# Routed expert blocks: conditional weight loads and stores, and a new pairing of blocks, in a four-layer kernel on one core

## Chip, core and metric

The kernel runs on one core of one Trainium2 chip. The metric is the device time of one execution in microseconds (us). Five engines work side by side: TensorE (PE, matmuls; its weight loads are shown as PEld), VectorE (DVE), ScalarE (ACT), GpSimd (POOL) and SyncE (SP, which here only issues DMAs). Each follows its own list of instructions and meets the others through semaphores. DMAs are issued from the queues of SP, ACT and POOL and move data between the large memory (HBM) and the on-chip memory (SBUF). A change is called a change here if it moves the time by more than about 1%, which is what a measurement of this kernel tells from no change.

## What is computed

The input is 8 sequences of 256 tokens with 256 features, 2048 tokens in all. Four layers follow each other, each inside `x = x + layernorm(layer(layernorm(x)))`: causal attention with 16 heads, a mixture of experts, an mLSTM, and a feed-forward layer with a 2:4 sparse hidden vector. The change lies in the mixture of experts:

```python
_, topk_idx = jax.lax.top_k(logits + router_bias, K)          # K = 4 of E = 64 experts
topk_scores = jnp.take_along_axis(scores, topk_idx, axis=-1)
topk_scores = topk_scores / (topk_scores.sum(-1, keepdims=True) + 1e-08)
combine = jnp.zeros((n, E)).at[jnp.arange(n)[:, None], topk_idx].add(topk_scores)
h = silu(einsum('nd,edf->enf', flat, Wg)) * einsum('nd,edf->enf', flat, Wu)     # F = 64
out = einsum('enf,efd->nd', h * combine.T[:, :, None], Wd)
for i in range(2):                                            # shared experts
    out = out + (silu(flat @ Sg[i]) * (flat @ Su[i])) @ Sd[i]
```

Only the 4 chosen experts of a token have a weight other than zero in `combine`, so 2048 x 4 = 8192 rows have to go through an expert.

## The kernel before, in words

All five engines' lists are written by hand, and no scheduler orders anything. The attention layer comes first (up to about 280 us of the profile), then the router and the shared experts, then the routed experts (363 to 580 us), then the mLSTM and the feed-forward layer.

**Blocks.** The router gives every expert as many blocks of 128 rows as its rows need. The blocks of all experts lie one behind the other, and there is room for XB = 128 of them. Block k belongs to expert `ebrow[k]`; `rows_at[:, k]` holds the token of each of its 128 rows, or a number outside the table where there is none. The blocks in use are the first ones; those behind are empty, and `ebrow` gives the last expert for them. How many are in use is known only at run time, in the last place of `upto`. For the inputs of the reference the rows per expert, counted from the reference's own formulas, make 96 blocks in use and 32 empty ones.

**Pairs.** The routed stage is a loop over XPAIR = 64 pairs of blocks, here called pair 0 to pair 63; pair i holds blocks 2i and 2i+1, so that pairs 0 to 47 are full and pairs 48 to 63 are empty. All 64 are computed in full. For each pair:

- SP loads the experts' weights, two DMAs of 192 KB (`expert_weights`, L405 and L406: read the expert's number from `ebrow` into a register, then issue). There are WRING = 7 buffers; the load for pair i waits until the second matmul step of pair i-7 is done (`e_dn`).
- POOL gathers the token rows, two indirect DMAs (L529), from `xnd` in HBM into a ring `xg` of RING = 4 pairs; the gathers for pair i wait for the transposes of pair i-4 (`e_xt`). Rows outside the table are not moved.
- PE transposes the rows (L1298, `e_xt`), ACT copies the result out of PSUM (L782, `e_xc`), PE does gate and up (L1310, `e_gu`), ACT takes the silu (L798, `e_sg`), DVE multiplies (L1999, `e_h`), PE does the down product (L1321, `e_dn`), DVE copies it to `ysb` (L2006, `e_y`).
- ACT stores the 256 rows of the pair to `yd` in HBM with one DMA of 256 KB (`expert_rows`, L787). `ysb` is a ring of 4 pairs: DVE's copy waits for the store of four pairs before (`e_o0` to `e_o3`).

PE's order is: transposes of i+1, gate and up of i, down of i-1. ACT's is: copy of i+1, silu of i, store of i-2.

After the loop POOL waits for all stores and gathers each token's four rows from `yd` (L545, the first at 583.9 us), while PE finishes the shared experts.

**Earlier on SP.** During the attention layer SP stores the normalized input of each sequence to `xnd` (L391, eight DMAs of 256 KB, the first at 87.6 us, the last at 276.0 us). The gathers wait for all eight (`x_st`).

## Time and profile before

| | us |
|---|---|
| three runs | 970.70, 972.15, 979.53 |
| their median | 972.15 |
| span of the profiled execution | 1017.7 |
| of it the stretch 363 to 580, the routed experts | 217 |

The profiled execution is an execution of its own and was 45.5 us longer than the median of the unprofiled ones. Share of the span in which each engine was busy: PE 85%, PEld 71%, DVE 66%, ACT 38%, POOL 39%. The granted clock of PE has the mean 0.892 of its full speed over the span.

How to read it: "busy" counts the engine's instructions, not its waits. A busy PE is not a PE at its best, because ends of matmuls are modelled. "Issue" is idle time in which the profile shows nothing that the engine waited for. The name behind an arrow is what ended the wait, "remote" or "another core or an unknown queue" one that the profile can't name.

### The profile page before, as it was taken

How to read it: one execution, taken by the hardware profiler on the slowest of the kernel's cores; microseconds unless marked ns; L12 is line 12 of the kernel's file. 1: busy time of each engine (PE TensorE's matmuls, PEld its weight loads, DVE VectorE, ACT ScalarE, POOL GpSimd, SP SyncE). 2: the span in 40 equal slices, each digit the busy share in tenths (PEclk: the TensorE clock that was granted, in tenths of full speed). 3: DMA queues.
4: the chain of work that ended last, by engine and by line, in shares of the span. 5: the costliest groups of instructions: out<-in, count | busy, mean ns of one | idle time of the engine just before them, and what ended most of it. 6: DMA issues, size and time to landing. Idle time of an engine off the chain costs nothing.

```text
span 1017.7 us, 18542 instructions
## 1 busy us (share of the span) xinstructions
PE 862.2 (85%) x6718; PEld 722.4 (71%) x6718; DVE 667.7 (66%) x1500; ACT 389.5 (38%) x764; POOL 396.7 (39%) x548
## 2 busy tenths in 40 slices
PE   4899899898688857667777859899999999999994
PEld 3777777776576846556666748778788888788883
DVE  6567777765577615885444547668778865867875
ACT  2244444444433713232222325435555564222220
POOL 3123333323432266766565283466665322100001
PEclk9799999998899968998898977758888887999997
DMA  7000000000000248888876551221111000000001
GB/s 248 2 1 13 12 12 9 5 12 12 22 1 22 87 136 260 250 257 242 242 222 184 162 178 52 82 59 52 46 42 41 0 1 1 0 1 21 22 1 41
DMA packets 59384, 77.66 MB, mean 76 GB/s; under 512 B 9746, under 2 KB 51997, under 8 KB 59304
## 3 DMA queue, kind: packets, MB, share of 16 engines
q1 hardware_dynamic: 32040, 40.92, 13.1%
q0 software_dynamic: 9856, 18.92, 6.9%
q10 hardware_dynamic: 17408, 16.78, 4.7%
q8 instruction: 47, 0.77, 0.3%
q14 instruction: 33, 0.27, 0.1%
HBM read 61.88 MB, written 23.07 MB: 83 GB/s over the span
## 4 chain that ended last, share of the span: by engine, by line
PE 43%; DVE 12%; issue 5%; another core or an unknown queue 4%; ACT 3%; POOL 2%; DMA 1%; ACTq 0%; POOLq 0%; DVEq 0%
PE S L1310 5%; PE S L1298 4%; PE S L959 3%; PE S L961 3%; PE S L960 3%; PE S L944 3%; PE ZO L1518 2%; PE ZO L1321 2%; PE T L1321 2%; PE T L1518 2%; PE ZO L1431 2%; DVE work L1566 1%; PE ZO L1433 1%; PE ZO L1432 1%
## 5 line engine op out<-in xcount | busy, mean ns | idle before, releaser
L529 POOL DMA_INDIRECT work<-xnd,rows_at x128 | 134.8, 1053 | 87.6 <-issue 38.6
L446 POOL TENSOR_SCALAR veps<-mv 128x2 f32<-128x2 f32 (+1 forms) x63 | 15.6, 247 | 287.8 <-DVE mv L1561 287.6
L1999 DVE TENSOR_TENSOR work<-work,S 64x256 f32<-64x256 f32 x128 | 54.2, 424 | 83.0 <-ACT work L798 52.9
L455 POOL TENSOR_SCALAR_AFFINE_SELECT work<-work 128x256 f32<-128x256 f32 x128 | 53.7, 444 | 118.0 <-ACT work L650 118.0
L959 PE MATMUL ZO<-parts 128*128 128x256 f32 x224 | 71.4, 319 | 16.6 <-DVE parts L1600 6.4
L959 PE MATMUL S<-xr,parts 128*128 128x512 f32 x192 | 83.5, 435 | 0.8 <-issue 0.8
L960 PE MATMUL S<-xr,parts 128*128 128x512 f32 x192 | 77.5, 404 | 0.0
L961 PE MATMUL S<-xr,parts 128*128 128x512 f32 x192 | 77.5, 403 | 0.0
L782 ACT ACTIVATE work<-S 128x512 f32<-128x512 f32 x64 | 38.2, 597 | 100.7 <-PE S L1298 43.5
L650 ACT ACTIVATE work<-S 128x768 f32<-128x768 f32 x64 | 51.7, 812 | 55.5 <-PE S L1033 55.5
L960 PE MATMUL ZO<-parts 128*128 128x256 f32 x224 | 66.3, 296 | 0.0
L961 PE MATMUL ZO<-parts 128*128 128x256 f32 x224 | 66.2, 295 | 0.0
L1033 PE MATMUL S<-parts 32*128 32x256 f32 (+1 forms) x768 | 57.9, 288 | 4.8 <-DVE parts L1626 3.8
L959 PEld LDWEIGHTS ZO<-parts 128*128 128x128 f32 x224 | 45.3, 202 | 21.9 <-issue 9.3
L1310 PE MATMUL S<-work,raw 128*128 128x128 f32 x296 | 46.7, 309 | 10.8 <-issue 10.7
L545 POOL DMA_INDIRECT attn_w<-yd,slots x44 | 49.8, 1131 | 11.9 <-issue 11.9
L1298 PE MATMUL S<-ident,work 128*128 128x128 f32 x256 | 47.4, 314 | 8.2 <-DMA work<-xnd,rows_at 8.2
L1033 PEld LDWEIGHTS S<-parts 32*128 32x128 f32 x768 | 48.9, 191 | 7.1 <-DVE parts L1626 5.0
L1310 PEld LDWEIGHTS S<-work,raw 128*128 128x128 f32 x296 | 42.5, 221 | 13.0 <-issue 12.9
L447 POOL TENSOR_TENSOR rstd<-veps,mhalf 128x2 f32<-128x2 f32 (+1 forms) x63 | 48.1, 763 | 5.2
L798 ACT ACTIVATE work<-S 64x256 f32<-64x256 f32 x64 | 24.1, 377 | 59.1 <-remote 30.8
L960 PEld LDWEIGHTS ZO<-parts 128*128 128x128 f32 x224 | 45.8, 205 | 0.1
(330 smaller groups left out, 2355.7 us busy)
## 6 DMA issues: line engine op xcount, KB each, us to landing
yd<-work ACTq DMA_DIRECT2D x64, 256.0 KB
raw<-in_experts SPq DMA_DIRECT2D x74, 192.0 KB
work<-in_experts SPq DMA_DIRECT2D x36, 192.0 KB
lg_all<-in_experts SPq DMA_DIRECT2D x18, 192.0 KB
xnd<-attn_w SPq DMA_DIRECT2D x8, 256.0 KB, 2.1
shd<-work SPq DMA_DIRECT2D x8, 256.0 KB, 2.3
work<-xnd,rows_at POOLq DMA_INDIRECT x128
raw<-in_ffn SPq DMA_DIRECT2D x2, 1024.0 KB, 5.4
```

The lines of the kernel that those rows point to most:

```text
L447: pool.tensor_tensor(rstd[:, 0:n], veps[:, 0:n], mhalf[:, 0:n], ALU.pow).then_inc(s["ln_rs"], 1)
L455: last = pool.affine_select(out=diagonal, in_=diagonal, compare_op=ALU.is_ge, fill=0.0, base=0, pattern=[[0, 2], [1, P]], channel_multipli ...
L529: pool.indirect_dma_start(xg[:, i % RING, b, :], None, xnd[:], bass.IndirectOffsetOnAxis(ap=rows_at[:, 2 * i + b:2 * i + b + 1], axis=0), ...
L545: pool.indirect_dma_start(gathered(b, t, k), None, yd[:], bass.IndirectOffsetOnAxis(ap=slots[:, 2 * b + t, k:k + 1], axis=0)).then_inc(s[" ...
L650: act.activation(pt[n % 6], SS[:, at:at + 1024].rearrange("p (r x) -> p r x", r=2)[:, :, 0:384], ACT.Exp).then_inc(s["a_exp"], 1)
L959: pe.matmul(dst, a(0), b(0), start=start, stop=False, skip_group_check=True)
L960: pe.matmul(dst, a(0), b(1), start=False, stop=False, skip_group_check=True)
L961: return pe.matmul(dst, a(1), b(0), start=False, stop=stop, skip_group_check=True)
L1033: return pe.matmul(bank[:, 2 * half * P:(2 + half) * P], side, top, start=k == 0 and half == 0, stop=k == 2, skip_group_check=True)
L1298: last = pe.transpose(S[i % 2][:, o:o + P], xg[:, i % RING, b, c * P:(c + 1) * P], ident[:])
L1310: last = pe.matmul(S[2 + i % 2][:, b * P:(b + 1) * P], pair_weights(i)[:, o:o + P], xT[:, i % 2, b, c, :], start=(c == 0), stop=(c == KC - 1))
L1999: last = dve.tensor_tensor(hx[64 * half:64 * half + 64, i % 2, :], sgx[64:128, i % 2, :], S[2 + i % 2][64:128, 0:256], ALU.mult)
```

## The change

Four things are changed.

1. Pair i holds block i and block 64 + (27 i + 13) mod 64 (`pair_blocks`), instead of 2i and 2i+1. The first is always in use here. The second runs once over the upper half, and with 96 blocks in use it is empty in 32 of the 64 pairs, spread over the loop (pairs 1, 4, 6, 8, 11, 13, 15, 16, 18, ... 60, 61, 63).
2. From pair 7 on, the load of the second block's weights carries a condition: it moves data only if the block is in use. 29 of the 128 loads are skipped. A skipped DMA still raises its semaphore.
3. The store of a pair is split into two DMAs of 128 KB, and the second carries the same condition. 32 of the 64 second stores are skipped. The waits on `e_o` count 32 for a pair instead of 16.
4. For the condition, the number of blocks in use is put into one more place of `ebrow` by a DVE copy and is read into a register once by SP and once by ACT. The rows of `yd` that may now never be stored are filled beforehand: behind the first four stores to `xnd`, SP issues a DMA of 2 MB that copies the input `x` within HBM into the upper half of `yd` (`y_base`; ACT waits for it before the loop and POOL before the gathers at the end).

Gathers, matmuls, copies and silus stay as many as before, also for empty blocks.

```diff
+        def pair_blocks(i):
+            return i, XPAIR + (27 * i + 13) % XPAIR
@@ SP
                 sp.dma_start(xnd[b * T:(b + 1) * T, :].rearrange("(t p) d -> p t d", p=P),
                              xn_all[:, 2 * b:2 * b + 2, :]).then_inc(s["x_st"], 16)
+                if b < 4:
+                    at = XPAIR * P + b * NT * P
+                    sp.dma_start(yd[at:at + NT * P, :], io["x"]).then_inc(s["y_base"], 16)
@@ expert_weights
-                for b in range(2):
-                    e = sp.value_load(ebrow[0:1, 2 * i + b:2 * i + b + 1], min_val=0, max_val=E - 1)
-                    sp.dma_start(pair_weights(i)[:, b * EW:(b + 1) * EW],
-                                 io["experts"][bass.ds(e, 1)].squeeze(0)).then_inc(pair_loaded(i)[0], 16)
+                for b, k in enumerate(pair_blocks(i)):
+                    e = sp.value_load(ebrow[0:1, k:k + 1], min_val=0, max_val=E - 1)
+                    sp.dma_start(pair_weights(i)[:, b * EW:(b + 1) * EW], io["experts"][bass.ds(e, 1)].squeeze(0),
+                                 cond=used > k if b and i >= WRING else None).then_inc(pair_loaded(i)[0], 16)
@@ SP, before the loads
+            used = sp.value_load(ebrow[0:1, XB:XB + 1], min_val=0, max_val=XB)
@@ POOL
-                for b in range(2):
+                for b, k in enumerate(pair_blocks(i)):
                     pool.indirect_dma_start(xg[:, i % RING, b, :], None, xnd[:],
-                                            bass.IndirectOffsetOnAxis(ap=rows_at[:, 2 * i + b:2 * i + b + 1], axis=0),
+                                            bass.IndirectOffsetOnAxis(ap=rows_at[:, k:k + 1], axis=0),
@@ POOL, after the loop
-                pool.wait_ge(s[f"e_o{k}"], 16 * (XPAIR // RING))
+                pool.wait_ge(s[f"e_o{k}"], 32 * (XPAIR // RING))
+            pool.wait_ge(s["y_base"], 64)
@@ expert_rows
-                act.dma_start(yd[i * 256:(i + 1) * 256, :].rearrange("(b p) d -> p b d", p=P),
-                              ysb[:, i % RING].rearrange("p b h d -> p b (h d)")).then_inc(s[f"e_o{i % RING}"], 16)
+                for b, k in enumerate(pair_blocks(i)):
+                    act.dma_start(yd[k * P:(k + 1) * P, :], ysb[:, i % RING, b].rearrange("p h d -> p (h d)"),
+                                  cond=used > k if b else None).then_inc(s[f"e_o{i % RING}"], 16)
@@ ACT, before the loop
+            act.wait_ge(s["r_eb"], 1)
+            act.wait_ge(s["y_base"], 64)
+            used = act.value_load(ebrow[0:1, XB:XB + 1], min_val=0, max_val=XB)
@@ block_table
+                dve.tensor_copy(ebrow[0:1, XB:XB + 1], upto[0:1, E - 1:E])
-                dve.tensor_copy(ebrow[:], S[3][0:1, 0:XB]).then_inc(s["r_eb"], 1)
+                dve.tensor_copy(ebrow[0:1, 0:XB], S[3][0:1, 0:XB]).then_inc(s["r_eb"], 1)
@@ DVE, before the copy to ysb
-                        dve.wait_ge(s[f"e_o{(i - 1) % RING}"], 16 * ((i - 1) // RING))
+                        dve.wait_ge(s[f"e_o{(i - 1) % RING}"], 32 * ((i - 1) // RING))
```

On ACT, this is the start of the loop before the change: the last copies of the shared experts (L747), then copies of transposed rows (L782), silus (L798) and the first store of a pair (L787).

```order
L747 ACTIVATE work<-T 128x512 [waits sh_o1]
L782 ACTIVATE work<-S 128x512 [waits e_xt,r_inv]
L782 ACTIVATE work<-S 128x512 [waits e_xt]
L798 ACTIVATE work<-S 64x256 [waits e_gu]
L782 ACTIVATE work<-S 128x512 [waits e_gu,e_xt]
L798 ACTIVATE work<-S 64x256 [waits e_gu]
L782 ACTIVATE work<-S 128x512 [waits e_gu,e_xt]
L798 ACTIVATE work<-S 64x256 [waits e_h,e_gu]
L787 DMA yd<-work 128x2x256 [waits e_y]
```

After the change it is this (the lines are now L756, L791, L811 and L797); the last three rows are those of the stores, further on in the loop.

```order
L756 ACTIVATE work<-T 128x512 [waits sh_o1]
L803 TENSOR_LOAD ebrow [waits y_base,r_eb,r_inv]
L803 ISA x2
L791 ACTIVATE work<-S 128x512 [waits e_xt] x2
L811 ACTIVATE work<-S 64x256 [waits e_gu]
L791 ACTIVATE work<-S 128x512 [waits e_gu,e_xt]
...
L811 ACTIVATE work<-S 64x256 [waits e_h,e_gu]
L797 DMA yd<-work 128x256 [waits e_y]
L797 ISA
L797 DMA yd<-work 128x256
```

A register load with its two register operations now stands ahead of the first copy, and behind each silu there are two stores with a register operation between them, where there was one store.

On SP, this is the stretch from the stores to `xnd` during attention to the first weight load, before the change (L397 stores rows of the shared experts).

```order
L388 DMA raw<-in_shared 128x768 x4
L391 DMA xnd<-attn_w 128x2x256 [waits a_xn2] x8
L397 DMA shd<-work 128x2x256 [waits f_rows] x4
L405 TENSOR_LOAD ebrow [waits r_eb,f_wl]
L405 ISA x2
```

After the change:

```order
L392 DMA raw<-in_shared 128x768 x4
L395 DMA xnd<-attn_w 128x2x256 [waits a_xn2]
L399 DMA yd<-in_x 32x16384
...
L395 DMA xnd<-attn_w 128x2x256 [waits a_xn2] x4
L404 DMA shd<-work 128x2x256 [waits f_rows] x4
L420 TENSOR_LOAD ebrow [waits r_eb,f_wl]
L420 ISA x2
L412 TENSOR_LOAD ebrow
```

The four copies of 2 MB stand one behind each of the first four stores to `xnd`, and one register load is added ahead of the first weight load. In the loop, SP's rows of a load are the same as before, with the condition inside the DMA instruction.

## Rows read from the trace of the kernel before

**Rows 1.** Busy time by stretch (us): engines with instruction counts, PE clock, DMA share, GB/s.

```profile
core 0: us, PE busy (x) PEld busy (x) DVE busy (x) ACT busy (x) POOL busy (x), PEclk, DMA share, GB/s
90.00:240.00 150.00, 135.51 (x1822) 109.80 (x1820) 109.23 (x273) 67.48 (x132) 47.72 (x111) 0.99 0.03 10
363.00:580.00 217.00, 160.60 (x1280) 137.47 (x1280) 122.61 (x219) 62.32 (x128) 130.64 (x125) 0.89 0.74 219
```

**Rows 2.** The same view inside the routed stage; full pairs end at about 527.

```profile
389.00:444.00 55.00, 39.15 (x339) 32.99 (x337) 42.40 (x65) 15.46 (x32) 38.30 (x34) 0.97 0.85 261
444.00:527.00 83.00, 59.23 (x478) 50.30 (x479) 45.45 (x88) 24.34 (x50) 51.47 (x50) 0.91 0.81 237
527.00:565.00 38.00, 29.97 (x228) 26.12 (x227) 17.05 (x34) 10.91 (x23) 21.71 (x23) 0.84 0.67 192
```

**Rows 3.** Line views of the transposes (L1298) and the gathers (L529), with a waiter.

```profile
L1298 PE MATMUL S<-ident,work x256: 272/273/477, 363.0 to 574.3; 128*128 128x128 f32 x128
...
L529 POOL DMA_INDIRECT work<-xnd,rows_at x128: 996/1002/2380, 357.9 to 567.1; - x128
...
  PE S L1298: 8.2, 2
```

**Rows 4.** Timeline of PE: transposes of pairs 48, 60, 62 and 63.

```profile
526.54 1.11 PE L1298 MATMUL S<-ident,work 128*128 128x128 f32 x4
...
566.23 0.66 PE L1298 MATMUL S<-ident,work 128*128 128x128 f32 x4
...
571.75 0.66 PE L1298 MATMUL S<-ident,work 128*128 128x128 f32 x4
...
573.87 0.66 PE L1298 MATMUL S<-ident,work 128*128 128x128 f32 x4
```

**Rows 5.** Timeline in the middle: two gathers, one behind the other.

```profile
473.21 1.00 POOL L529 DMA_INDIRECT work<-xnd,rows_at  x1 [0.30 <-issue]
...
474.52 1.00 POOL L529 DMA_INDIRECT work<-xnd,rows_at  x1 [0.30 <-issue]
```

**Rows 6.** Timeline of one stop of PE, ACT and DVE.

```profile
487.49 1.06 PE L1310 MATMUL S<-work,raw 128*128 128x128 f32 x8
...
489.53 0.60 ACT L782 ACTIVATE work<-S 128x512 f32<-128x512 f32 x1 [2.89 <-remote]
...
493.90 0.38 ACT L798 ACTIVATE work<-S 64x256 f32<-64x256 f32 x1 [3.77 <-remote]
...
494.31 0.86 DVE L1999 TENSOR_TENSOR work<-work,S 64x256 f32<-64x256 f32 x2 [5.59 <-ACT work L798]
```

**Rows 7.** The chain that ended last: two pieces (start us, us, what).

```profile
489.56 4.32 another core or an unknown queue
...
593.79 7.56 another core or an unknown queue
```

**Rows 8.** Waits in 363 to 580: us in total, times, longest us.

```profile
ACT work L798 <- remote: 30.8, 11, 3.8
```

**Rows 9.** Gather queue in 444 to 520, then in 530 to 565: packets, MB, share.

```profile
q0 software_dynamic: 2197, 3.66, 20.6%
...
q0 software_dynamic: 961, 0.01, 1.7%
```

**Rows 10.** Line views of SP's loads and ACT's store: ns min/median/max.

```profile
L405 SPq TENSOR_LOAD <-ebrow x128: 3/276/1052, 340.3 to 565.3; - x128
L405 SPq FUSED_REGOPS  x128: 3/152/685, 341.1 to 565.6; - x128
...
L787 ACTq DMA_DIRECT2D yd<-work x64: 366/367/428, 378.8 to 580.0; - x64
```

**Rows 11.** The block table's copy on DVE; ACT's first copy of the loop.

```profile
L1879 DVE CAST ebrow<-S x1: 271/271/271, 338.1 to 338.1; 1x128 int32<-1x128 f32 x1
...
364.21 0.60 ACT L782 ACTIVATE work<-S 128x512 f32<-128x512 f32 x1 [8.79 <-issue]
```

**Rows 12.** SP's stores to `xnd` during attention.

```profile
L391 SPq DMA_DIRECT2D xnd<-attn_w x8: 359/360/382, 87.6 to 276.0; - x8
```

More of the change, by code:

```diff
@@ L88, in build @@
         wtop = sb("wtop", [P, NT, TOPK])
-        ebrow = sb("ebrow", [1, XB], mybir.dt.int32)
+        ebrow = sb("ebrow", [1, XB + 1], mybir.dt.int32)
         eye1 = sb("eye1", [P, H1])
@@ L309, in build @@
             f_g f_u f_sg f_h f_hh f_hl f_wh f_wl f_blk f_rows
-            x_st r_zero r_oh r_im r_inv sh_o0 sh_o1 e_xt e_xc e_gu e_sg e_h e_dn e_y e_w0 e_w1 e_w2 e_w3 e_x0 e_x1 e_x2 e_x3
+            x_st y_base r_zero r_oh r_im r_inv sh_o0 sh_o1 e_xt e_xc e_gu e_sg e_h e_dn e_y e_w0 e_w1 e_w2 e_w3 e_x0 e_x1 e_x2 e_x3
             e_o0 e_o1 e_o2 e_o3 m_in m_in1 m_add
```

## The prediction

> **What bounds the kernel now.** I read the views in this order. First the busy time by stretch: the change touches one stage, the 64 pairs, which fills 363 to 580, 217 of 1017.7 us. The DMA engines are busy for 0.74 of it and next to idle (0.03) in the attention stretch [rows 1]. So the question is what sets the pace of a pair. The first transposes stand at 363.0 and the last pair's at 573.87 [rows 3, 4]: 210.9 us for 63 steps, 3.35 us each.
>
> Then I compare this with what each engine needs. PE: where nothing disturbs it, the transposes of two pairs stand at 571.75 and 573.87, 2.12 us apart [rows 4]. POOL: a gather takes 1.00 us and 0.30 us of issue ahead of it, and two in a row start 1.31 us apart [rows 5]; two a pair make 2.60 us, and POOL pays this for an empty block too. DVE is busy for 42.4 of 55 us where it has most to do [rows 2]. ACT needs 0.60 + 0.38 for copy and silu [rows 6] and 0.37 for the store [rows 10], 1.35 us. The highest need is POOL's, 64 x 2.60 = 166 us, against 211 us that the loop took. The other 45 us are no engine's work.
>
> Where they are is shown by waiters and a timeline. The rows are not late: PE's transposes waited for a gather twice, for 8.2 us in all [rows 3]. What is late is the word that PE has finished. PE's rows put the gate and up of a pair at 487.49 to 488.55. ACT has nothing else to do from 490.13 on, yet its silu of that result starts at 493.90, after 3.77 us, and DVE has then waited 5.59 us [rows 6]. The chain can't name what ended 4.32 us there [rows 7]. ACT's silus waited like that 11 times, 30.8 us in all, 3.8 at most [rows 8].
>
> The profiled execution is 1017.7 - 972.15 = 45.5 us longer than the median, and the loop's excess over POOL's pace is of the same size. I infer, and no row shows it, that in the unprofiled runs the loop goes at about POOL's pace and that the stops belong mostly to the profiled execution.
>
> **The change part by part.** The sum is made against the profiled loop and carried to the median.
>
> *Bytes removed.* 29 loads of 192 KB and 32 stores of 128 KB are 9.9 of 50.3 MB. Before, a full pair moves 393 KB of weights, 262 KB of stores and 175 KB of gathered rows (8192 rows of 1 KB over 48 pairs), 830 KB; an empty pair moves 655 KB. Afterwards the mean pair moves 632 KB. Lower bound of the gain: nothing, as no engine waits for loads and POOL's work stays. Upper bound, at POOL's pace: in stretches of full pairs the DMA engines moved 261 GB/s at a share of 0.85 and 237 at 0.81 [rows 2], which extended to a full share is 307 and 293, say 300. A full pair then takes 830/300 = 2.77 us, 0.17 over 2.60, and 48 of them give 8 us. Afterwards 632/300 = 2.11 us is under what PE and POOL need. I take 5 us, nearer to the upper bound, because those stretches are near full share already at a pace below POOL's.
>
> The Trainium skill, page "DMA: Bandwidth & Descriptors", section "Specifications", gives a limit of about 358 GB/s from HBM for a core. By that a full pair would take 2.32 us, DMA would never set the pace, and this term would be 0 instead of 5 us. No stretch in rows 2 went over 261 GB/s, so the sum goes by the rows.
>
> *A row that speaks against more.* Behind pair 47 all blocks are empty: the gather queue moved 0.01 MB in 530 to 565, against 3.66 MB in 444 to 520 [rows 9]. Such a pair carries nearly what the mean pair will carry. Yet pairs 48 to 60 took from 526.54 to 566.23, 3.31 us each [rows 4]. Fewer bytes alone did not quicken the profiled loop.
>
> *The second store on ACT.* One more issue of 0.37 us and a register operation of 0.15 [rows 10] with small steps between: 0.55 us a pair. ACT goes from 1.35 to 1.9 us, under POOL's 2.60 and PE's 2.12. Behind the store on ACT stands the next copy, and PE's gate and up of a later pair waits for that copy; PE has a down product and transposes to do meanwhile. Cost 0. With that cover gone it is 64 x 0.55 = 35 us.
>
> *Waits on the stores.* DVE waits for the store of four pairs back, 10 us at POOL's pace, and two smaller ones move no more bytes. 0.
>
> *Register loads and the DVE copy.* A TENSOR_LOAD takes 0.28 us, 1.05 at most [rows 10]. ACT's lies in its idle 8.79 us ahead of the loop [rows 11]. SP's delays the first weight load, 20 us before it is used. The added DVE copy is at most the 0.27 us of the old one [rows 11]. Together 0.3 us at most; I take 0.
>
> *The four copies of 2 MB.* They are issued behind the first four of eight stores between 87.6 and 276.0 us [rows 12], on average 27 us apart, where DMA is at 0.03 [rows 1]. At 237 to 261 GB/s each takes 8 to 9 us in one direction, 16 to 18 for read and write. 0, with rival C as the upper bound.
>
> *Conditions on SP.* The instructions stay as many as before. 0.
>
> Sum: 972.15 - 5 = 967 us, and 1013 for a profiled execution like the one before.
>
> **The rivals.**
>
> *A. The stops are real and go with the traffic.* Then the loop runs at 3.35 us in the unprofiled runs too, and fewer loads and stores make the stops fewer. For it: stops of this kind show where DMA is busy. Against it: the empty pairs at 3.31 us, and one such piece of 7.56 us at 593.79 [rows 7], when the loop's loads and stores had ended. Price: by bytes 20% of 45 us, 9 us; at most all 45. I take half, 22: 950 us.
>
> *B. ACT becomes the pace (slower).* At their maxima the register operation takes 0.69 and the issue 0.43 us [rows 10], with small steps 1.25 together. ACT would then need 1.35 + 1.25 = 2.6 us, the point from which it decides. With 0.2 us a pair over it, 64 x 0.2 = 13 us: 985 us. For it: the maxima come from SP while it issues with DMA as busy as here. Against it: the medians, and less traffic afterwards.
>
> *C. The copies disturb attention (slower).* PE is busy for 135.5 of 150 us there [rows 1], so what stops it costs in full. If each copy brings one stop of 4 us as in rows 7, the sum is +16 us: 983 to 988 us. Against it: they are few large pieces, and no engine works on what they move.
>
> *D. The loads are skipped and nothing comes of it,* as POOL's 128 gathers stay: 972 us. It is the upper part of the likeliest case.
>
> **How the numbers follow.** The likeliest case (POOL's pace, small relief, D included) has 0.55, its own range is 960 to 976, its time 967. A has 0.30, B 0.09, C 0.06. The range from 944 to 983 leaves out the part of A below 944 (0.10) and of B and C above 983 (0.08). Faster by over 1% is below 962.4: A and 0.05 of the likeliest case, 0.35. Slower by over 1% is above 981.9: two thirds of B and C, 0.10. Within 1%, which is about what a measurement of this kernel can tell from no change: 0.55.
>
> **What would show it.** In the profile afterwards: a DMA share of the loop below 0.65; gathers still 1.30 us apart; two issues on ACT behind a silu within 0.6 us; the stores to `xnd` at 87.6 and 276.0 as now. A loop well below 3.3 us a pair together with a median of 950 or less would show A right and my inference on the stops wrong. PE's gate and up waiting for ACT's copy while ACT is at its second store would show B. A later last store to `xnd` would show C.

## The result and the profile after

| | before | after |
|---|---|---|
| median of 20 runs each (us) | 974.87 | 971.22 |
| lowest, highest | 970.15, 982.61 | 967.57, 976.15 |
| ratio, 95% interval | | 0.9964, 0.9948 to 0.9979 |
| span of the profiled execution | 1017.7 | 970.5 |

The change takes 3.5 us off (2.0 to 5.1), 0.4%: real, and under the 1% that counts as a change here. The forecast was 967 us, 5 under the 972.15 it started from. 2.7 us of the 4.2 between 967 and 971.22 are the starting point: 20 runs of before have the median 974.87, and the three that I had lay lower. The rest is the term of the bytes, forecast at 5; it measured 3.5 if the other terms were the 0 that they were put at.

The profiled execution of before was 45.5 us longer than its median, that of the changed kernel is 970.5 us. So the first question is what the kernel before looks like without its stops. It was profiled once more, unchanged (experiment e1_again): span 971.4 us. In what follows "before" in a comparison of traces is this second execution; its lines have the numbers of the kernel before.

Busy time by stretch, first of the second execution of before, then of after (columns as in [rows 1]):

```profile
90.00:240.00 150.00, 136.94 (x1796) 109.98 (x1796) 107.68 (x270) 66.05 (x130) 47.09 (x110) 0.98 0.03 10
363.00:540.00 177.00, 144.89 (x1272) 125.60 (x1272) 120.79 (x217) 62.30 (x128) 130.72 (x126) 0.95 0.87 269
```

```profile
90.00:240.00 150.00, 135.47 (x1821) 109.97 (x1822) 109.22 (x273) 67.40 (x132) 47.48 (x110) 0.99 0.17 60
363.00:540.00 177.00, 144.44 (x1287) 125.13 (x1287) 122.54 (x219) 62.42 (x129) 128.75 (x124) 0.97 0.73 215
```

The routed stage fills 363 to 540 in both, not 363 to 580 as in [rows 1]. The DMA engines are relieved by a fifth, from 269 to 215 GB/s, and PE, DVE and ACT do in the same 177 us the same work within 2%. The four copies show in the attention stretch as 60 instead of 10 GB/s, and PE is as busy there as before.

The line views of the gathers (ns min/median/max, first and last start; indented below the second, who waited for them: us, times), before and after:

```profile
L529 POOL DMA_INDIRECT work<-xnd,rows_at x128: 994/999/2547, 359.3 to 530.8; - x128
```

```profile
L537 POOL DMA_INDIRECT work<-xnd,rows_at x128: 997/1002/2007, 357.4 to 528.2; - x128
...
  PE S L1311: 26.3, 21
```

From the first to the last gather it is 171.5 us before and 170.8 after: the pace of the loop did not move. It is POOL's: 128 gathers at 1.34 us, and 1.30 is the least that two in a row take [rows 5]. In both timelines 114 of the 127 steps from one gather to the next are 1.33 us or less; the 13 longer ones all start ahead of 449 us. Before, the full pairs' gathers up to 489 us and the empty pairs' behind them go at the same 1.30. The waits of the stage (us in total, times, longest) say the same, before and then after:

```profile
ACT work L782 <- PE S L1298: 97.2, 64, 9.1
...
PE S L1298 <- DMA work<-xnd,rows_at: 34.9, 36, 6.7
...
ACT work L798 <- PE S L1310: 23.1, 64, 1.4
```

```profile
ACT work L791 <- PE S L1311: 99.1, 62, 8.9
...
PE S L1311 <- DMA work<-xnd,rows_at: 26.3, 21, 6.7
ACT work L811 <- PE S L1323: 14.8, 41, 1.4
```

PE waits for gathered rows 36 and 21 times, where [rows 3] had 2 waits. And no wait of ACT is put down to "remote" any more, where [rows 8] had 30.8 us: a silu now waits 1.4 us at most for its gate and up, against 3.8.

ACT's line of the stores has 128 issues, the skipped ones being the short ones, with a register operation for every second:

```profile
L797 ACTq DMA_DIRECT2D yd<-work x128: 102/338/1274, 371.8 to 538.5; - x128
L797 ACTq FUSED_REGOPS  x64: 144/144/172, 372.3 to 538.3; - x64
```

SP's stores to `xnd` and the copies behind them, with the time to landing of the copies:

```profile
L395 SPq DMA_DIRECT2D xnd<-attn_w x8: 359/367/380, 87.3 to 275.7; - x8
```

```profile
L399 SPq DMA_DIRECT2D yd<-in_x x4: 521/818/1348, 87.7 to 176.8; - x4
...
DMA to landing us min/median/max: 8.6/9.1/9.3
```

**Where the gain is.** Both traces are alike up to the last gather; they part behind it. This is the timeline of POOL and of ACT at the end of the loop, before (start us, duration, engine and line, idle before it):

```profile
530.84 1.00 POOL L529 DMA_INDIRECT work<-xnd,rows_at  x1 [0.30 <-issue]
...
545.70 1.01 POOL L545 DMA_INDIRECT attn_w<-yd,slots  x1 [0.30 <-issue]
```

```profile
536.38 0.60 ACT L782 ACTIVATE work<-S 128x512 f32<-128x512 f32 x1 [0.85 <-PE S L1298]
...
539.29 2.89 ACTq L787 DMA_DIRECT2D yd<-work  x3
```

And after:

```profile
528.21 1.00 POOL L537 DMA_INDIRECT work<-xnd,rows_at  x1 [0.30 <-issue]
...
541.47 1.01 POOL L553 DMA_INDIRECT attn_w<-yd,slots  x1 [0.30 <-issue]
```

```profile
532.18 0.60 ACT L791 ACTIVATE work<-S 128x512 f32<-128x512 f32 x1 [1.45 <-PE S L1311]
...
535.10 3.54 ACTq L797 DMA_DIRECT2D yd<-work  x6
```

Before, ACT's copy of the last pair starts 5.5 us behind the issue of the last gather (530.84 to 536.38), after it 4.0 us (528.21 to 532.18). And POOL's first gather from `yd`, which needs all stores landed, starts 3.9 us behind the issue of the last store (it was at 541.81), after it 2.9 us (last at 538.54, one that is skipped). The two together are 2.5 us. Pair 63 has an empty second block, so the very last store moves nothing. The stage as a whole is 2.4 us shorter: there are also 0.8 us less between the first and the last gather, and 0.9 us more between the last copy and the last store.

The 5.5 us are not one landing time. In this trace PE waited for the rows of pair 59 and then ran at the lower of its two clock levels for a while, and the last transposes (at 535.68) waited for nothing but PE's own work. PE's timeline before, and the row of 527 to 529 us, where the granted clock is 0.50:

```profile
525.64 0.66 PE L1298 MATMUL S<-ident,work 128*128 128x128 f32 x4 [2.08 <-DMA work<-xnd,rows_at]
...
528.71 1.11 PE L1298 MATMUL S<-ident,work 128*128 128x128 f32 x4
...
531.43 0.66 PE L1298 MATMUL S<-ident,work 128*128 128x128 f32 x4
```

```profile
527.00:529.00 2.00, 2.00 (x13) 1.55 (x13) 0.89 (x3) 0.38 (x1) 1.70 (x2) 0.50 0.75 204
```

From 525.64 to 531.43 two pairs took 5.79 us instead of 2 x 2.12, so about 1.6 us of the 5.5 are the clock. Over the last ten pairs the copy starts 5.4 us behind the pair's second gather before, 4.6 after and 3.1 in e3_conditions (experiment 3). Outside the stage the two traces differ by more than the effect (behind it they take 425.7 and 429.0 us), and their spans by 0.9 us only. So the traces show where time falls away inside the stage, but not how the 3.5 us of the medians are made up.

The table gives these stretches for all kernels of this study, each from one profiled execution (us): first to last gather from `xnd`; last of them to ACT's last copy; issue of the last store to the first gather from `yd`; first gather from `xnd` to first gather from `yd`, which is the whole stage. Before, e2, e4 and e8 leave the traffic of the last pairs in place; they spread by 1.0 us in the third column and by 1.3 us in the stage. A difference of that size between two traces shows nothing. The fourth column is steadier: 3.7 to 4.0 us where the last store moves all its bytes, 2.9 where half of it is skipped (after, e11) and 1.9 to 2.1 where all of it is (e3, e5, e12); e13 and e14 stand apart. e9 and e12 have no gathers behind pair 47, hence the 41 and 39 us in the third column.

| kernel | gathers | to last copy | store to `yd` gather | stage | ratio of medians, 95% |
|---|---|---|---|---|---|
| before (e1_again) | 171.6 | 5.5 | 3.9 | 186.4 | 1 |
| after | 170.8 | 4.0 | 2.9 | 184.0 | 0.9964, 0.9948 to 0.9979 |
| e2_pairing | 172.1 | 5.2 | 3.9 | 186.7 | 1.0016, 0.9983 to 1.0048 |
| e3_conditions | 171.5 | 3.1 | 1.9 | 182.6 | 0.9955, 0.9925 to 0.9985 |
| e4_split | 171.8 | 4.7 | 3.7 | 186.1 | 1.0016, 0.9988 to 1.0043 |
| e5_tail8 | 170.8 | 3.8 | 1.9 | 182.4 | 0.9978, 0.9949 to 1.0006 |
| e6_head8 | 171.9 | 3.6 | 3.7 | 185.2 | 0.9972, 0.9945 to 0.9998 |
| e7_loads_only | 171.5 | 3.4 | 4.0 | 184.3 | 0.9974, 0.9947 to 1.0001 |
| e8_copies | 171.7 | 4.5 | 3.9 | 185.4 | 1.0023, 0.9993 to 1.0054 |
| e9_skip_before | 131.8 | 41.4 | 4.0 | 183.8 | 0.9935, 0.9901 to 0.9969 |
| e10_skip_pairing | 156.5 | 9.3 | 3.9 | 176.0 | 0.9896, 0.9865 to 0.9927 |
| e11_skip_after | 149.1 | 7.6 | 2.9 | 166.3 | 0.9776, 0.9750 to 0.9802 |
| e12_skip_cond | 129.4 | 39.1 | 2.1 | 176.6 | 0.9880, 0.9845 to 0.9915 |
| e13_branch | 168.1 | 5.2 | 5.9 | 185.6 | 0.9954, 0.9929 to 0.9978 |
| e14_branch_skip | 150.0 | 8.3 | 4.5 | 169.2 | 0.9790, 0.9755 to 0.9825 |

### The profile page after: what moved, and what is told of

The parts are those of the page before. It is cut to its first block and busy times, and to the rows that moved or that the text cites. A ratio compares the mean times of both kernels' runs of the same rounds, so it can differ in the third digit from the quotient of the medians.

```text
span 970.5 us, 18748 instructions
## 1 busy us (share of the span) xinstructions
PE 836.4 (86%) x6718; PEld 704.0 (73%) x6718; DVE 667.2 (69%) x1501; ACT 389.3 (40%) x764; POOL 394.9 (41%) x548
## 5 line engine op out<-in xcount | busy, mean ns | idle before, releaser
L791 ACT ACTIVATE work<-S 128x512 f32<-128x512 f32 x64 | 38.2, 598 | 100.9 <-PE S L1311 99.1
L1311 PE MATMUL S<-ident,work 128*128 128x128 f32 x256 | 43.1, 292 | 26.4 <-DMA work<-xnd,rows_at 26.3
L972 PEld LDWEIGHTS ZO<-parts 128*128 128x128 f32 x224 | 45.3, 202 | 21.6 <-issue 9.3
L1311 PEld LDWEIGHTS S<-ident,work 128*128 128x128 f32 x256 | 27.9, 145 | 36.0 <-DMA work<-xnd,rows_at 24.1
L973 PEld LDWEIGHTS ZO<-parts 128*128 128x128 f32 x224 | 45.8, 204 | 0.1
L974 PEld LDWEIGHTS ZO<-parts 128*128 128x128 f32 x224 | 45.8, 204 | 0.0
L2190 DVE TENSOR_TENSOR work<-work,S 128x512 f32<-128x512 f32 x32 | 21.9, 685 | 34.2 <-ACT work L927 23.6
```

Source lines behind the costliest of these rows:

```text
L972: pe.matmul(dst, a(0), b(0), start=start, stop=False, skip_group_check=True)
L973: pe.matmul(dst, a(0), b(1), start=False, stop=False, skip_group_check=True)
L974: return pe.matmul(dst, a(1), b(0), start=False, stop=stop, skip_group_check=True)
L1311: last = pe.transpose(S[i % 2][:, o:o + P], xg[:, i % RING, b, c * P:(c + 1) * P], ident[:])
```

## The experiments

**1. The kernel before, profiled once more.** No edit.

> The kernel before, unchanged, profiled once more. Theory 1 (the stops belong to that one profiled execution and not to the kernel's usual run): the loop of 64 pairs takes 2.65 to 2.8 us a pair and the span is about 972 us. Rival (the stops come with the kernel before whenever it is profiled, and the change removes them): a span near 1017 us with several waits of 3.8 us of ACT's silu in the loop.

Measured: 973.39 us, span 971.4. The stops do not come back. They belonged to that one profiled execution, and the 3.35 us a pair of the prediction's first step was no property of the kernel. That inference, for which the prediction had no row, is now shown, and rival A falls with it.

**2. The new pairing alone.** All loads and stores stay, one store of 256 KB a pair, no copies.

```diff
+        def pair_blocks(i):
+            return i, XPAIR + (27 * i + 13) % XPAIR
@@ SP and POOL: the numbers of ebrow and rows_at
-                for b in range(2):                       # block 2 * i + b
+                for b, k in enumerate(pair_blocks(i)):
@@ ACT
-                act.dma_start(yd[i * 256:(i + 1) * 256, :].rearrange("(b p) d -> p b d", p=P),
+                lo, hi = pair_blocks(i)
+                act.dma_start(yd[:].rearrange("(n p) d -> p n d", p=P)[:, lo:hi + 1:hi - lo, :],
```

> Only the new pairing; loads and the one 256 KB store of a pair stay unconditional, no copies. It moves as many bytes as before but spreads the gathered rows: 786 KB in every pair instead of 830 in 48 and 655 in 16. Theory 1 (POOL's 2.60 us a pair is the pace, and DMA is over it only in full pairs): most of the gain is here, 2 to 5 us faster than before (ratio 0.995 to 0.998). Rival (the gain comes from bytes not moved): no difference, ratio 0.999 to 1.001.

Measured 974.71 us, ratio 1.0016. The spreading of the empty blocks shows no gain by itself; the interval leaves room for 1.7 us. It was expected to bring 2 to 5 us, which missed.

**3. The conditions alone, with the old pairing.** Everything of the change but the pairing, the four copies included; now both blocks of a pair can be empty, so both carry the condition.

```diff
-            return i, XPAIR + (27 * i + 13) % XPAIR
+            return 2 * i, 2 * i + 1
@@ SP
-                                 cond=used > k if b and i >= WRING else None).then_inc(pair_loaded(i)[0], 16)
+                                 cond=used > k if i >= WRING else None).then_inc(pair_loaded(i)[0], 16)
@@ ACT
-                                  cond=used > k if b else None).then_inc(s[f"e_o{i % RING}"], 16)
+                                  cond=used > k).then_inc(s[f"e_o{i % RING}"], 16)
```

> Only the conditions, with the pairs as before (2i, 2i+1), both loads and both stores of a pair conditional, copies included: 32 loads and 32 stores skipped, all in pairs 48 to 63, which are under POOL's pace anyway. Theory 1: no difference, ratio 0.999 to 1.001. Rival (bytes not moved): as fast as the whole change, ratio 0.996.

Measured 968.2 us, ratio 0.9955: the whole gain of the change, perhaps a little more. I had expected none, since full pairs keep their bytes. With this run and the one before, the gain is in the bytes that are not moved, not in where the empty blocks lie. The stretches of full pairs are as loaded as ever: from 450 to 500 the DMA engines have a share of 0.98 in the kernel before, and the gathers are 1.31 us apart all the same. Here is that row, and then the last 40 us of the loop:

```profile
450.00:500.00 50.00, 41.12 (x379) 35.41 (x378) 29.82 (x58) 18.12 (x39) 38.36 (x39) 1.00 0.98 307
```

```profile
500.00:540.00 40.00, 34.85 (x310) 30.17 (x308) 23.74 (x48) 14.76 (x31) 24.52 (x25) 0.96 0.75 221
```

The same 40 us of e3_conditions:

```profile
500.00:540.00 40.00, 33.41 (x307) 29.05 (x308) 24.97 (x49) 14.01 (x29) 24.33 (x25) 1.00 0.06 16
```

POOL does 25 gathers in both, so 0.75 or 0.06 of traffic is the same to its pace. What differs lies behind the gathers and the stores: the last copy stands 5.5 and 3.1 us behind the last gather (some of it the clock, as said above), the `yd` gather 3.9 and 1.9 us behind the last store (table). The stage is 3.8 us shorter; the medians say 4.4, between 1.5 and 7.3.

**4. Two stores instead of one.** The kernel before with its store split into two of 128 KB.

```diff
-                act.dma_start(yd[i * 256:(i + 1) * 256, :].rearrange("(b p) d -> p b d", p=P),
-                              ysb[:, i % RING].rearrange("p b h d -> p b (h d)")).then_inc(s[f"e_o{i % RING}"], 16)
+                for b in range(2):
+                    k = 2 * i + b
+                    act.dma_start(yd[k * P:(k + 1) * P, :], ysb[:, i % RING, b].rearrange("p h d -> p (h d)")
+                                  ).then_inc(s[f"e_o{i % RING}"], 16)
```

> Only the stores split into two DMAs of 128 KB, unconditional: the price of 64 more issues on ACT. Theory 1 (hidden under POOL's pace): ratio 0.999 to 1.001. Rival B (it lies on the path): up to 64 x 0.4 = 26 us slower, ratio 1.005 to 1.026.

Measured 974.32 us, ratio 1.0016, at most 4 us (1.0043): hidden, as the prediction had it. Rival B with its 13 us falls.

**5 to 7. Which of the removed bytes count.** After experiment 3 there were two theories: "last landing" (POOL keeps the pace, bytes matter only for what lands last) and "bytes" (DMA is part of the pace, bytes matter everywhere). e5 and e6 remove the same number of bytes, once in the last eight pairs and once ahead of them; e7 removes the loads alone.

```diff
@@ e5_tail8, against e3_conditions (loads and stores alike)
-  cond=used > k
+  cond=used > k if i >= XPAIR - 8 else None
@@ e6_head8
+  cond=used > k if WRING <= i < XPAIR - 8 else None    # loads
+  cond=used > k if i < XPAIR - 8 else None             # stores
@@ e7_loads_only, against the kernel before
-                                 io["experts"][bass.ds(e, 1)].squeeze(0)).then_inc(pair_loaded(i)[0], 16)
+                                 io["experts"][bass.ds(e, 1)].squeeze(0),
+                                 cond=used > 2 * i + b if i >= WRING else None).then_inc(pair_loaded(i)[0], 16)
```

> The kernel before with its own pairing (blocks 2i and 2i+1), the stores split and the four copies, and conditions on loads and stores only in the last 8 pairs, 56 to 63, all empty: 16 loads and 16 stores are skipped. Theory 'last landing': POOL's gathers set the pace of the loop (first to last 171.5 us in the kernel before as profiled again, with e3_conditions and, within 0.7, after the change), and the gain comes only from the end: in the last four pairs ACT's copy starts 6.2 us behind the issue of the second gather, with the conditions 3.1 us, and POOL's first gather of yd starts 3.9 us behind the issue of the last store, with the conditions 1.9. It expects nearly all of the gain of e3_conditions: 970 us, ratio 0.995 to 0.997, and the gathers still 171.5 us from first to last. Theory 'bytes', that DMA is part of the pace wherever it is busy: half the bytes, half the gain, ratio 0.9975 to 0.9985, the same as e6_head8.

> As e5_tail8, but the conditions stand in all pairs except the last 8: of the empty pairs it is 48 to 55, so again 16 loads and 16 stores are skipped, as many bytes as in e5_tail8, but nothing of the end. Theory 'last landing': the last stores move their bytes again and POOL waits 3.6 to 3.9 us behind their issue; the last gathers land beside less traffic than in the kernel before, up to 1 us of gain there. Ratio 0.999 to 1.001. Theory 'bytes': 0.9975 to 0.9985, as e5_tail8.

> The kernel before, its pairing, one unconditional store of 256 KB a pair, no copies; only the weight loads are conditional (the 32 of pairs 48 to 63). 6.3 of 50.3 MB are removed. Theory 'last landing': the half that lies in the landing of the last gathers comes (up to 2 us of 3.1), the half at the last store does not (3.9 us behind its issue as before): 972.5 us, ratio 0.9975 to 0.999. Theory 'bytes': 6.3 of 10.4 MB, 60% of the gain of e3_conditions: 0.997 to 0.998. If the loads alone give all of it, 0.9955.

Measured: 970.9, 970.05 and 970.88 us, ratios 0.9978, 0.9972 and 0.9974, each with an interval of 0.6% in width. The times do not tell the theories apart: e6 was to be at 0.999 to 1.001 by the first and 0.9975 to 0.9985 by the second, and its interval reaches from 0.9945 to 0.9998. The traces tell part of it (table). The gathers take 170.8, 171.9 and 171.5 us, so none of the three wins anything in the pace, which speaks against "bytes". The wait behind the last store is 1.9 us where the last stores are skipped and 3.7 and 4.0 where they are not, as "last landing" had it. The stage is shorter by 4.0, 1.2 and 2.1 us, which is the order that it expected, but the 1.2 of e6 are within the 1.3 by which like kernels differ. And e6, whose last eight pairs move all their bytes, has its last copy 3.6 us behind the last gather, sooner than any of the kernels with unchanged traffic (4.5 to 5.5): that part of "last landing" is not borne out.

**8. The four copies alone.**

```diff
+                if b < 4:
+                    at = XPAIR * P + b * NT * P
+                    sp.dma_start(yd[at:at + NT * P, :], io["x"]).then_inc(s["y_base"], 16)
@@ ACT, before the loop
+            act.wait_ge(s["y_base"], 64)
```

> The kernel before plus only the four copies of 2 MB from x into the upper half of yd, and ACT's wait for them ahead of the loop. My prediction: hidden, ratio 0.9985 to 1.0015. Rival C of the prediction: the attention layer is disturbed, up to 16 us, ratio 1.015.

Measured 975.46 us, ratio 1.0023 (0.9993 to 1.0054). The middle is 2 us, and 5 are not excluded; rival C's 16 is out. No trace shows a cost: PE is busy for 136.1 us of the attention stretch against 136.9, and the first gather of the loop starts between 354.2 and 360.7 us in the nine kernels with the copies and between 354.8 and 362.0 in the six without.

The changed kernel has no version without the copies: rows of `yd` would be read that nothing had written.

**9 to 12. POOL's empty gathers taken away.** If POOL's gathers hide the relief, then taking away the 32 gathers of empty blocks must bring it out. The count of 96 is fixed in these kernels, so they are right for these inputs only. The edit is the same in all four, applied to before, e2_pairing, after and e3_conditions:

```diff
+        USED = 96
+        def gathered_blocks(i):
+            return [(b, k) for b, k in enumerate(pair_blocks(i)) if k < USED]
@@ POOL
-                for b, k in enumerate(pair_blocks(i)):
+                for b, k in gathered_blocks(i):
@@ PE: the count of e_x follows the gathers that there are
-                pe.wait_ge(s[f"e_x{i % RING}"], 32 * (i // RING + 1))
+                pe.wait_ge(s[f"e_x{i % RING}"], gather_count(i))
```

> The kernel before without the 32 gathers of its empty blocks (pairs 48 to 63), left out by a fixed count of 96 blocks, right for these inputs; loads and stores as before. If POOL's gathers are the pace, pairs 48 to 63 go at what is next: PE's 2.12 us or, with 655 KB at 300 GB/s, DMA's 2.2 us, instead of 2.7: 16 x 0.5 = 8 us less, ratio 0.990 to 0.994. If DMA is the pace already, at most 0.998.

> e2_pairing (new pairing, all loads and stores) without the 32 gathers of empty blocks, which are now spread over the loop. POOL needs 96 x 1.34 = 129 us instead of 171, PE 64 x 2.12 = 136. If DMA stands close behind POOL as my term of the bytes had it (a mean pair of 786 KB at 300 GB/s takes 2.62 us, 168 us in all), it becomes the pace and takes nearly the whole gain: 0 to 4 us, ratio 0.996 to 1.000. If DMA is nowhere near the pace, the loop goes towards PE's 136 us: over 20 us, ratio under 0.98.

> The changed kernel without the 32 gathers of empty blocks. A mean pair moves 632 KB, 2.11 us at 300 GB/s. With POOL at 129 us and PE at 136 the loop should take 140 to 155 us instead of 171: 16 to 30 us less, ratio 0.970 to 0.984. That is: the conditions are worth over 12 us beside e10_skip_pairing, where POOL no longer covers the traffic. If POOL isn't the pace after the change, nothing beyond 0.996.

> e3_conditions (old pairing, conditions on all loads and stores) without the 32 gathers. Pairs 0 to 47 stay full and keep POOL's pace; only 48 to 63 go at PE's 2.12 us: 16 x 0.55 = 9 us, and the end 4 us as in e3_conditions, 13 in all: ratio 0.985 to 0.989. The new pairing would then be worth 5 to 15 us (e11_skip_after beside this one), since it gives every second pair a gather less. If the pairing is worth nothing, both come out the same.

Measured, with and without the 32 gathers (medians in us). The right column is of one set of runs, in which the kernel before had the median 974.25. The left one is of two others: the changed kernel's 971.22 stands against 974.87, the other three against 974.02.

| | all gathers | 32 left out |
|---|---|---|
| before | 974.0 | 967.46 |
| new pairing | 974.71 | 963.38 |
| old pairing, conditions | 968.20 | 964.57 |
| new pairing, conditions (the change) | 971.22 | 952.53 |

Three of the four fell into their ranges; e10 was expected at 0 to 4 us and brought 10 (ratio 0.9896), about half of what its rival theory asked for. The change is worth 3.5 us as it stands. Where POOL is relieved, the conditions are worth 10.9 us (963.38 to 952.53) and the new pairing 12.0 (964.57 to 952.53). Pairing without conditions runs into DMA. From 450 to 490, e10 and then e11:

```profile
450.00:490.00 40.00, 37.59 (x344) 32.37 (x343) 26.36 (x52) 16.52 (x34) 25.14 (x26) 1.00 0.97 312
```

```profile
450.00:490.00 40.00, 40.00 (x377) 35.18 (x377) 28.67 (x56) 18.26 (x38) 27.63 (x28) 1.00 0.88 267
```

In e10 the DMA engines are at 0.97 and 312 GB/s and PE isn't always busy: its gate and up (L1326) now waits for weights. In the kernel before it has no such wait in 400 to 515; in e10 it has these (us, times, longest):

```profile
PE S L1326 <- DMA raw<-in_experts: 3.0, 4, 1.7
PE S L1326 <- DMA lg_all<-in_experts: 1.1, 1, 1.1
PE S L1326 <- DMA work<-in_experts: 0.4, 1, 0.4
```

Behind the longest of them, at 497.17, PE's clock falls as above: the next transposes take 1.11 us instead of 0.66. In e11 these waits are 1.0 us in all. PE is busy for 40.00 of 40 us and is the pace, at the 2.12 us of [rows 4], and POOL now waits for PE's transposes (us, times), where in the changed kernel PE waited for POOL:

```profile
  PE S L1322: 25.2, 21
```

e9 and e12 show the same by place: pairs 48 to 63, whose gathers fell away, take 2.28 and 2.15 us each instead of 2.61, and pairs 0 to 47 keep their 2.7.

**13. A kernel that is right for any routing: a branch, and a small gather for an empty block.**

```diff
+            used = pool.value_load(ebrow[0:1, XB:XB + 1], min_val=0, max_val=XB)
@@ POOL, second block of a pair
+                    pool.cond(used > k, gather, lambda: gather(16))     # gather(rows): the first rows places only
```

> The changed kernel, right for any routing: POOL reads the number of used blocks into a register, and for the second block of each pair it branches on it: a full gather if the block is in use, else a gather of only 16 rows, all outside the table, which raises the same semaphore. No row here shows what a branch or a gather of 16 rows costs on POOL. If the 1.00 us of a gather goes with its rows, POOL gets back up to 32 x 0.9 = 28 us less the branches, and with a branch under 0.3 us (64 x 0.3 = 19 us) PE becomes the pace as in e11_skip_after: ratio 0.978 to 0.985. If a gather costs 1.00 us whatever its rows, POOL's work stays 171 us plus the branches: ratio 0.997 to 1.02. In both cases POOL's pace alone decides, since conditions and pairing are those of the changed kernel.

Measured 969.83 us, ratio 0.9954, as the changed kernel (its own 0.9964). Two gathers in its timeline, the first with 16 rows:

```profile
442.83 0.90 POOL L540 DMA_INDIRECT work<-xnd,rows_at  x1 [0.30 <-issue]
444.03 1.03 POOL L540 DMA_INDIRECT work<-xnd,rows_at  x1 [0.31 <-issue]
```

A gather of 16 rows takes 0.90 us, one of 128 takes 1.00. So POOL pays for the instruction, not for the rows, and a smaller gather wins next to nothing. The branch shows no cost here: the issue ahead of a gather is 0.30 us with it as without. The gathers take 168.1 us instead of 170.8, about 32 x 0.10 less, but the stage is 185.6 us long against 184.0: POOL starts on `yd` 5.9 us behind the last store instead of 2.9, and the last copy is 1.2 us later behind the last gather. I had bounded the outcome at 0.997 to 1.02 for this case; 0.9954 is below it, and its interval (0.9929 to 0.9978) holds both the bound and the changed kernel's 0.9964.

**14. Right for any routing, and no gather for an empty block.** The gathers of second blocks get semaphores of their own, and POOL and PE both branch. The semaphores of the kernel were all in use, so four of the last layer's share those of the attention layer, whose final count is known.

```diff
-            return i, XPAIR + (27 * i + 13) % XPAIR
+            return i, XPAIR + i // 2 + (i % 2) * (XPAIR // 2)
@@ POOL
+                    if b:
+                        pool.cond(used > k, gather, lambda: None)      # raises e_z, not e_x
+                    else:
+                        gather()
@@ PE, before the transposes
-                pe.wait_ge(s[f"e_x{i % RING}"], 32 * (i // RING + 1))
+                pe.wait_ge(s[f"e_x{i % RING}"], 16 * (i // RING + 1))
+                pe.cond(used > pair_blocks(i)[1],
+                        lambda: pe.wait_ge(s[f"e_z{i % RING}"], 16 * (i // RING + 1)), lambda: None)
```

> Right for any routing, and no gather at all for an empty second block. The gathers of the second blocks have semaphores of their own (e_z); POOL branches past a gather whose block is empty, and PE, which reads the number of used blocks too, branches past the wait for it. So that a semaphore's count is known ahead of time, the second blocks of a ring place come in rising order: pair i takes block 64 + i//2 if i is even, 96 + i//2 if it is odd (here every second pair has an empty one, as nearly in the changed kernel). e13_branch showed that a gather of 16 rows takes 0.90 us on POOL and that its branches add nothing to the 1.30 us pitch: the cost is in the instruction. If that is so, this kernel comes to e11_skip_after: ratio 0.976 to 0.982. Against it: PE is the pace then, and 64 branches on its sequencer with the wait split off could cost 0.05 to 0.2 us each, 3 to 13 us: ratio 0.982 to 0.990. Nothing beyond 0.996 if POOL's instructions are not the pace.

Measured 954.3 us, ratio 0.9790 (0.9755 to 0.9825): 20 us under the kernel before and, by the two ratios, 17 under the changed one. It beats both, without a fixed count. That a kernel is right for any routing is argued here and in 13 from its code; only the inputs with 96 blocks ran. Its gathers, two of them with a skipped one between, and the same 40 us of the loop:

```profile
L542 POOL DMA_INDIRECT work<-xnd,rows_at x96: 992/998/1540, 360.7 to 510.7; - x96
```

```profile
457.31 1.00 POOL L542 DMA_INDIRECT work<-xnd,rows_at  x1 [0.30 <-issue]
458.95 1.00 POOL L542 DMA_INDIRECT work<-xnd,rows_at  x1 [0.65 <-issue]
```

```profile
450.00:490.00 40.00, 39.40 (x369) 34.58 (x369) 28.18 (x55) 17.93 (x38) 27.18 (x28) 1.00 0.88 263
```

PE is busy for 39.40 of 40 us, against 40.00 in e11, so its branches cost at most 0.6 us in these 40. How this kernel does with other counts of used blocks was not measured.

## Why the prediction was right or wrong

**The pace of a pair: right.** POOL's two gathers set it, the stops were the profiled execution's, and both are now measured (171.6 us before, 170.8 after; experiments 1, 9, 11, 14).

**Bytes removed, -5 us: the step that failed.** The sum laid this gain on the pace: DMA would hold POOL's 2.60 us back by 0.17 in each of 48 full pairs. It does not. In the stretch with a DMA share of 0.98 the gathers keep their 1.30 to 1.31 us, and with a fifth of the bytes gone the same 128 gathers take 170.8 us instead of 171.5. What the runs show in its place: the gain comes with the bytes (e3: 0.9955) and not with the pairing (e2: 1.0016), and the part of it that the traces show clearly lies once, at the end of the stage, where POOL's wait behind the last store falls from 3.9 to 2.9 us in the changed kernel and to 1.9 in e3. The last copy, too, is sooner behind the last gather, by 1.5 us in the two traces, but kernels with the same traffic differ by 1.0 there and the lower clock has a share in it.

The measured size is 3.5 us (2.0 to 5.1), about a third under the 5. It is a net size: e4 and e8 leave room for 4 and 5 us that the second store and the copies may cost. That it comes out near 5 is luck, since the mechanism that gave the 5 was absent. The rate of 300 GB/s was not far off (307 at a share of 0.98). At 307 a full pair takes 2.70 us against the 2.61 at which the gathers go, 4 us in 48 pairs, and weights are loaded up to seven pairs ahead, so DMA can fall behind by that much without anyone waiting. The sum had no buffers in it. That they take up the deficit is argued from these numbers, and no run tested it.

**The Trainium skill's rule that was weighed there.** The Trainium skill, page "DMA: Bandwidth & Descriptors", section "Specifications", gives a limit of about 358 GB/s for a core. By that the term was 0, since DMA would never set the pace. As to the pace it came out so before and after the change; but e10 is held back by DMA, its PE waiting for weights, at 312 GB/s. The highest that a stretch of 40 us or more showed here is 312, nearer to my 300 than to the rule's figure.

**The row that spoke against more** was the better guide: in the first profile the empty pairs were no faster than the full ones. Without the stops it still holds: by the first and last transposes of each part, pairs 0 to 47 take 2.75 us each in e1_again and pairs 48 to 63 take 2.61, but nearly all of the 0.14 comes from the 13 long steps between gathers ahead of 449 us, and the changed kernel has them too. Full pairs behind 449 go at 2.61.

**Second store on ACT, 0: right.** e4_split, ratio 1.0016. The second store starts about 0.6 us behind the first; with both it is 0.96 us of issue a pair, or 0.71 where the second is skipped, against 0.37 before, which is the 0.55 of the prediction within 0.2. Only at the very end does nothing hide it, in the 0.9 us more from the last copy to the last store.

**Register loads, DVE copy, conditions, waits on stores, 0: right** as far as the gathers' 171 us show; none was measured by itself.

**Four copies, 0: not refuted,** within -1 to 5 us. They take 9 us each to land, about 230 GB/s, where 16 to 18 had been worked out by counting a copy within HBM once for the read and once for the write.

**Rivals.** A (stops go with traffic) fell in experiment 1, B in 4, C in 8. D, "nothing comes of it", was priced at 972 and lies nearest to the 971.22 measured; but against 974.87, 3.5 us did come of it, clear of the noise.

**The signs it named:** gathers 1.30 us apart and the `xnd` stores at the same places held. The two stores' issues start about 0.6 us apart. The DMA share was to be below 0.65 and is 0.73: it had been set against the 0.74 of the 217 us of [rows 1], and in the stretch without stops it falls from 0.87.

**The starting point.** The median of three runs lay 2.7 us under that of twenty. With a spread of 10 us between runs this is ordinary, and it was nearly as large as the effect. A forecast of so small a gain can't be told right or wrong by its time alone.

**What stays open.** How the 3.5 us are made up. That they lie at the end of the stage rests on single traces, of which only the wait behind the last store (1.0 us of it) repeats from kernel to kernel; the medians of e5, e6 and e7 cannot tell it from an even spread. What makes the 13 steps ahead of 449 us long was not looked into; DVE is at its busiest there. In e13 and e14 POOL starts on `yd` 5.9 and 4.5 us behind the last store instead of 2.9; what it does in the 1.6 to 3.0 us more was not found.

## What to carry to other kernels

Relief on a resource that is not the pace is worth little, however many transfers it removes: look for it at the last transfers of a stage, and at what waits for them. Then take away what covers the relief: here an instruction that costs 1.0 us with or without rows. The whole change was worth 3.5 us with it; without it the conditions alone were worth 11. And profile the kernel a second time before its waits are explained: 45 us of this first profile were in no other execution.

## What the runs showed of the hardware

- A gather on POOL costs 0.90 us for 16 rows and 1.00 us for 128, with 0.30 us of issue ahead of it, also where no row is inside the table. A branch on a register between two gathers adds nothing to the issue when both paths hold a gather, and 0.35 us to the issue where the gather is branched past (0.65 instead of 0.30).
- A DMA whose condition is false raises its semaphore and its issue takes 0.10 us on ACT (lowest value above) and 0.08 on SP, instead of 0.34 and 0.33, with a register operation of 0.14 and 0.04 us ahead of it. SP's line in the changed kernel:

```profile
L413 SPq FUSED_REGOPS  x128: 42/42/204, 341.6 to 523.2; - x128
...
L413 SPq DMA_DIRECT2D raw<-in_experts x74: 84/333/378, 341.7 to 523.5; - x74
```

- The DMA engines moved 307 to 312 GB/s at a share of 0.97 to 0.98, and ACT's copy of a pair then started 4.8 to 6.4 us behind the issue of its last gather (e1_again, 450 to 500 us), against 2.8 to 3.6 in the last ten pairs of e3_conditions, where there was next to no other traffic.
- In e1_again PE stood still for 2.08 us, and from 527 to 529 us its granted clock was 0.50, the lower of the two levels (1.2 of 2.4 GHz); four transposes took 1.11 us instead of 0.66. In the changed kernel a stop of 2.14 us, at 481, was followed by no such fall.
- One profiled execution ran with stops of 4 us and was 45.5 us over its median. None of the 15 later ones, of the changed kernel and of the fourteen experiments, is more than 9 us from its own.
